# Low passes of a split matrix product moved behind the transposes of the next norm, in a fused two-layer cross-attention and mixture-of-experts kernel

## The chip, the cores and the metric

The kernel runs on one core of a Trainium2 chip. The metric is the device time of one execution in microseconds (us). Each kernel is timed in several runs, and the median counts.

## The reference

The input `x` has 2 x 1024 rows of 256 numbers, the context 2 x 64 rows of 192. Two layers follow one another, each an attention over the context and a feed-forward part, each on a normalised input and with a residual. Cut to what matters here:

```python
x = x + _L0_xattn_ref(_layernorm(x), ctx, ...)   # 16 heads; then relu(out @ W1 + b1) @ W2 + b2
x = x + _L0_ffn_ref(_layernorm(x), ...)          # below
x = x + _L1_xattn_ref(_layernorm(x), ctx, ...)   # one head
x = x + _L1_ffn_ref(_layernorm(x), ...)          # linear

def _L0_ffn_ref(hidden_states, wi, bi, wo, bo, lora_A, lora_B, gate_w, gate_b):
    scores = jax.nn.softmax(hidden_states @ gate_w.T + gate_b)     # 8 experts
    top_v, top_i = jax.lax.top_k(scores, 2)
    val_sum = top_v.sum(axis=-1)
    for e in range(8):
        gate = (top_i == e).sum(axis=-1) * val_sum
        inter = x @ wi.T + bi + (x @ lora_A[e].T) @ lora_B[e].T    # 256 -> 1024
        out = out + gate[..., None] * (relu(inter) @ wo.T + bo)    # 1024 -> 256
    return out
```

All of it is float32.

## The kernel before

The 2048 rows are cut into 8 blocks (`NBLK`) of 256 rows, each of two tiles of 128 rows (`NT` = 2). A block passes through stages that are named by letters: `h` and `a`, the first attention (norm 1, queries, row maxima; then scores, attention, hidden layer and its output), `f`, the expert part (norm 2, gate, hidden layer, output), and `c`, the second layer (norms 3 and 4). One round, `body(a, f, c, h)`, works on four blocks at once: `a` is the round's own block, `f` the block before it, `c` the one before that, and `h` the next one. There are eight rounds, `a` = 0 to 7; round 0 has no `f` and no `c`, round 1 no `c`, and round 7 no `h`. After them come `drain` and `end` for what is left of the last blocks.

Each engine has its own instruction stream, written out by hand in the same round structure; there is no scheduler. The streams meet at semaphores: `pe.wait_ge(S("hidl"), n)` holds back the instruction that follows, and with it all that stands behind it on TensorE. So the order of the lines in `body` of the tensor block is the order on TensorE.

Float32 products are made of three passes over split operands: each operand is stored as a high part of reduced precision (`_h`, type fp32r) and a low part (`_l`, the remainder), and high x high, high x low and low x high are added up in PSUM. The high part is made by ScalarE, the low part by VectorE or GpSimd, as a subtraction.

The names that the change and the steps of the prediction touch:

- `f_out(f, t)` (L474): the second projection of the experts, 1024 -> 256, for tile `t` of block `f`. The activations `HH`, `HL` (`hid_h`, `hid_l` in the profile) are loaded as weights, `wo` streams. `high=True` gives its two passes with `hid_h` (8 matmuls with `wo_h`, 8 with `wo_l`; `NFF` = 8), `low=True` the pass with `hid_l` (8 matmuls). All of it adds up in one PSUM bank, `I_(0)`, half a bank for each tile. The first call waits for `hidh` (ScalarE, L849), the low pass for `hidl` (GpSimd `sum_low`, L1447). The last low pass signals `x2_ps`.
- `second_residual(f)` (VectorE, L1140) waits for `x2_ps` and makes X2; `c_turn(f)` (L490, transposes at L496) waits for X2 and for VectorE's `z`. `f_base(a, 0)` (L450) comes after it. In round 1 (`f == 0`) TensorE also waits for `vv_l` before `c_turn`, a subtraction of VectorE (L1336) that stands between `low(2, a)` and `second_residual(f)` in its queue.
- `a_row_scores(h, t)` (L356): two matmuls of 512 columns for the row maxima of tile `t` of the next block. Those of tile 1 use the same banks as those of tile 0, and so wait for `mx`, VectorE's `row_max(h, 0)` (L1069).
- `a_out(a, half)` (L408): the output of the first layer's hidden part; its end signals `x1_ps`, on which VectorE makes the first residual and the statistics of norm 2 (L1082, L1042 to L1053). GpSimd's `scale(2, a)` then takes the power (L1428) and the product `nmr` (L1432), and ScalarE's `normalise(2, a)` writes `xn`, one tile at a time (L791). `scale(2, a)` stands behind `sum_low(f, 2)` and `sum_low(f, 3)` in GpSimd's queue.
- `transposes(2, a)` (L326): four transposes of `xn`, two for each tile, each pair behind a wait for that tile's `ln2_xh`. ScalarE then makes the high part `xtf_h` (L796), VectorE the low part `xtf_l` (L1057).
- `a_max_transposes(h)` (L365): one transpose of the row maxima; it waits for both row maxima.
- `f_gate(a, h)` (L420, passes at L311 with 136 columns): the gate and the low-rank projections of block `a`, the first user of `xtf_h` and `xtf_l`.
- `experts(a)` on VectorE (L1084 to L1109) ends in `am`, for which `f_lora_transposes` (L434) waits in the next round.

In VectorE's queue the order here is `hidden_sum(f, 3)`, `queries_low(h)`, `row_max(h, 0)`, `first_residual(a)` with the statistics of norm 2, `fourth_residual(c)` (L1183), `row_max(h, 1)`, `low(2, a)`, `second_residual(f)`, statistics of X2, `experts(a)`.

Of the kernel before, what the change touches and what calls it, by code (L numbers as in the profile page):

```python
# [59 lines left out]
def build(nc, io):  # L60
# [157 lines left out]
    with block:  # L218
# [74 lines left out]
        def _(pe):  # L293
# [12 lines left out]
            def passes(parts, chunks, pairs, start, stop):  # L306

                for a, b in pairs:
                    for i, (out, lhs, rhs) in enumerate(parts):
                        for k, c in enumerate(chunks):  # L310
                            last = mm(out, lhs(a, c), rhs(b, c), start=start and (a, b) == pairs[0] and i == 0 and k == 0,  # L311
                                      stop=stop and k == len(chunks) - 1, skip_group_check=True)
                return last

            def w(name, m, n=P):

                return lambda a, c: (WH, WL)[a][name][:, c, m:m + n]

            def x_of(halves, lo=0, n=T):
                return lambda a, c: halves[a][:, c, lo:lo + n]  # L320
# [46 lines left out]
            def a_scores(b, d):  # L367

                if d == 0:
                    if b % BPB == 0:  # L370
                        pe.wait_ge(S(f"ks{b // BPB}"), 16 * 3)
                        pe.wait_ge(S("ks_ind"), b // BPB + 1)
                    for r in range(3):
                        pe.wait_ge(S(f"qstack{r}"), (b + 1) * 16 * GPC)
                    pe.wait_ge(S("mstack"), (b + 1) * NT)
                if d >= 2:
                    pe.wait_ge(S("ex"), b * DPAIRS + d - 1)
                for k in range(2):
                    last = mm(S_(d % 2)[:, k * T:(k + 1) * T], KS[:, b // BPB * PAIRS + 2 * d + k, :],  # L379
                              QS[:, 2 * d + k, :], start=True, stop=True)  # L380
                last.then_inc(S("sc"), 1)

            def a_attend(b, m):

                if m == 0 and b % BPB == 0:
                    pe.wait_ge(S("v0_ready"), b // BPB + 1)
                    pe.wait_ge(S("ld_kept"), 16)
                at = b // BPB * D
                for d in (2 * m, 2 * m + 1):
                    pe.wait_ge(S("ex"), b * DPAIRS + d + 1)  # L390
                    for c in (2 * d, 2 * d + 1):
                        rows = slice(PW * (c % GPC), PW * (c % GPC) + PW)
                        mm(P_(m)[rows, 0:T], v0[:, at + c * PW:at + (c + 1) * PW], EX[:, c, :], start=True, stop=True)  # L393
                        last = mm(P_(m)[rows, T:2 * T], ones_pair, EX[:, c, :], start=True, stop=True)  # L394
                last.then_inc(S("pv"), 1)
# [35 lines left out]
            def f_lora_transposes(b):  # L431
                pe.wait_ge(S("am"), b + 1)
                for k in range(2 * NT):
                    last = nc.tensor.transpose(P_(0)[:, k * P:(k + 1) * P], am[:, k * P:(k + 1) * P], ident)  # L434
                last.then_inc(S("amT"), 1)
# [26 lines left out]
            def f_first(b, u, bank=None):  # L462
                if u == 0:
                    if b == 0:
                        pe.wait_ge(S("lo_w"), 5)
                    pe.wait_ge(S("atl"), b + 1)
                f_lora(b, u, 0, "first_ps", bank)
# [6 lines left out]
            def f_out(b, t, high=True, low=True):  # L474

                if t == 0:
                    if b == 0:
                        pe.wait_ge(S("lo_wp"), 4)
                    pe.wait_ge(S("hidh"), (b + 1) * NDF)
                part = [(I_(0)[:, t * D:(t + 1) * D], x_of((HH, HL), t * P, P), w("wo", 0, D))]  # L480
                if high:
                    passes(part, range(NFF), ((0, 0), (0, 1)), t == 0, False)
                if low:
                    pe.wait_ge(S("hidl"), (b + 1) * NDF)
                    last = passes(part, range(NFF), ((1, 0),), False, True)
                    if t == NT - 1:
                        last.then_inc(S("x2_ps"), 1)
# [15 lines left out]
            def c_scores(b, t):  # L503

                if t == 0:
                    if b == 0:
                        pe.wait_ge(S("gw_l"), 1)
                    split_in(3, b)
                three(T_(t)[:, 0:SY], x_of(XTC, t * P, P), folded_weights(b), range(KC)).then_inc(S("sc1_ps"), 1)
# [108 lines left out]
            def filler(bank, count):  # L618
                for _ in range(count):
                    mm(bank[:, 0:T], zeros[:, 0:P], zeros[:, :], start=True, stop=True)  # L620
# [38 lines left out]
            def body(a, f, c, h):  # L659
                A_, F_, C_, H_ = (v is not None for v in (a, f, c, h))  # L660
                if A_:
                    a_scores(a, 0)
                    a_scores(a, 1)
                if F_:
                    f_lora_transposes(f)
                if C_:
                    c_scores(c, 0)
                    c_scores(c, 1)
                if F_:
                    f_first(f, 0)  # L670
                    f_first(f, 1)
                if A_:
                    a_scores(a, 2)
                if a == 0:
                    filler(I_(0), 2)
                if A_:
                    a_attend(a, 0)
                if F_:
                    f_second(f, 0)
                if f == 0:  # L680
                    fold_means()
                if C_:
                    c_transpose(c)
                if F_:
                    f_second(f, 1)
                if A_:
                    a_scores(a, 3)
                if F_:
                    f_base(f, 2)
                if C_:  # L690
                    c_attend(c)
                if A_:
                    a_attend(a, 1)
                if F_:
                    f_first(f, 2)
                    f_base(f, 3)
                    f_second(f, 2)
                    f_first(f, 3)
                if a == 0:
                    filler(I_(0), 3)  # L700
                    pe.wait_ge(S("v0"), BATCH)
                    transposes(1, h, T_(1))
                    filler(I_(0), 5)
                if A_:
                    a_hidden(a, 0)
                if H_ and a > 0:
                    if f == 0:
                        pe.wait_ge(S("gw"), 1)
                    if C_:
                        pe.wait_ge(S("z"), (c + 1) * NT)  # L710
                    transposes(1, h, T_(1))
                if A_:
                    a_hidden(a, 1)
                if H_:
                    a_queries(h)
                if f == 0:
                    fold_values()
                if F_:
                    f_second(f, 3)
                if A_:  # L720
                    a_out(a, 0)
                if H_:
                    a_row_scores(h, 0)
                if A_:
                    a_out(a, 1)
                if F_:
                    f_out(f, 0)
                if H_:
                    a_row_scores(h, 1)
                if F_:  # L730
                    f_out(f, 1, low=False)
                if a == 0:
                    constant_row()
                    keys1()
                    values1()
                if A_:
                    transposes(2, a, T_(1))
                if a == 0:
                    folded_keys()
                if F_:  # L740
                    f_out(f, 1, high=False)
                if H_:
                    a_max_transposes(h)
                if A_:
                    f_gate(a, h)
                    if a == 0:
                        pe.wait_ge(S("v1"), 1)
                        pe.wait_ge(S("gb"), 1)
                        fold_turn()
                    if F_:  # L750
                        if f == 0:
                            pe.wait_ge(S("vv_l"), 2)
                        c_turn(f)
                    f_base(a, 0)
                    f_base(a, 1)
                elif F_:
                    c_turn(f)
# [860 lines left out]
```

## Time and profile before

| | |
|---|---|
| median of 3 timed runs | 330.58 us |
| lowest and highest | 329.61, 331.83 us |
| time of the profiled execution | 332.24 us |
| its span, first to last instruction | 330.1 us |
| mean granted clock of TensorE | 0.988 |
| busy: TensorE matmuls, weight loads | 314.6 us (95%), 285.6 us (87%) |
| busy: VectorE, ScalarE, GpSimd | 231.2, 173.7, 146.2 us |

The profile is of one execution. PE is TensorE's matmuls, PEld its weight loads, which overlap the matmuls; DVE is VectorE, ACT ScalarE, POOL GpSimd. L311 is line 311 of the kernel; for a helper that many callers share (L302, L311, L458) the tile names tell the stage. A matmul is reported with its whole passage through the array, so matmuls that follow each other overlap in the profile: the distance between the starts of two groups of weight loads tells better than the durations how long a group holds TensorE. The ends of matmuls are modelled.

### The profile page before, as it was taken

The page shows a single profiled execution, that of the slowest core. Times are in us where ns is not written, and L with a number is a line of the kernel's source. Part 1 is how long each engine was busy: PE and PEld are TensorE (multiplying, and loading weights), DVE is VectorE, ACT ScalarE, POOL GpSimd, SP SyncE. Part 2 cuts the span into 40 slices and gives each one's busy share as a digit, 9 for nine tenths or more (in the row PEclk, how much of TensorE's full clock was granted, in tenths as well). Part 3 has the DMA queues.
Part 4 walks back from the last instruction along what each step waited for, and adds up shares of the span by engine and source line. Part 5 has one row for each costly group of instructions (what it writes and reads, how often), then busy time and mean ns, then how long its engine had stood idle before and what let it go on. Part 6 is the DMA issues. An engine that isn't in the chain of part 4 may idle for free.

```text
span 330.1 us, 6479 instructions
## 1 busy us (share of the span) xinstructions
PE 314.6 (95%) x2497; PEld 285.6 (87%) x2497; DVE 231.2 (70%) x644; ACT 173.7 (53%) x355; POOL 146.2 (44%) x150
## 2 busy tenths in 40 slices
PE   7989998999999999999999999999999999999982
PEld 5748897899988999899989997999899988999771
DVE  4746676747878667956886687677786669456766
ACT  3346746572585456564667267635854564534411
POOL 2563681636053723654173607280537234613341
PEclk9989999999999999999999999999999999999997
DMA  8589720003100230013000410032002200000000
GB/s 244 156 247 359 165 82 0 2 9 89 32 3 2 57 92 13 2 26 104 36 0 10 96 57 0 2 85 77 2 0 50 69 13 1 2 0 34 0 34 32
DMA packets 14702, 18.85 MB, mean 57 GB/s; under 512 B 2224, under 2 KB 11312, under 8 KB 14416
## 3 DMA queue, kind: packets, MB, share of 16 engines
q1 hardware_dynamic: 12640, 14.99, 16.9%
q10 hardware_dynamic: 2032, 3.44, 3.0%
q8 instruction: 20, 0.33, 0.4%
q14 instruction: 10, 0.08, 0.1%
HBM read 9.51 MB, written 2.62 MB: 37 GB/s over the span
## 4 chain that ended last, share of the span: by engine, by line
PE 76%; POOL 8%; ACT 5%; DVE 5%; DMA 2%; SPq 2%; issue 1%; DVEq 0%; POOLq 0%; ACTq 0%
PE psI L302 13%; PE psI L458 12%; PE psI L311 9%; PE psP L311 7%; PE psS L311 7%; PE psT L302 4%; POOL hid_l L1447 4%; PE psP L393 3%; POOL hs_l L1441 3%; PE psS L379 2%; PE psT L326 2%; PE psP L394 2%; PE psT L525 2%; ACT qu_h L801 2%; PE psI L620 1%; ACT hs_h L829 1%
## 5 line engine op out<-in xcount | busy, mean ns | idle before, releaser
L1428 POOL TENSOR_TENSOR rs<-ve,mhalf 128x2 f32<-128x2 f32 x30 | 22.3, 745 | 95.3 <-DVE ve L1053 95.3
L1447 POOL TENSOR_TENSOR hid_l<-r,hid_h 128x512 fp32r<-128x512 f32 x32 | 40.8, 1288 | 15.3 <-ACT hid_h L849 15.3
L1132 DVE SCALAR_TENSOR_TENSOR r<-psI,nbi,r 128x256 f32<-128x256 f32 x60 | 25.8, 479 | 25.3 <-PE psI L458 25.2
L458 PE MATMUL psI<-at_h,lb_h 128*128 128x256 f32 x120 | 36.5, 304 | 2.1 <-DVE at_l L1124 1.5
L1441 POOL TENSOR_TENSOR hs_l<-hs,hs_h 128x512 fp32r<-128x512 f32 x16 | 20.8, 1301 | 35.6 <-ACT hs_h L829 35.4
L458 PE MATMUL psI<-at_l,lb_h 128*128 128x256 f32 x120 | 33.9, 282 | 0.0
L458 PE MATMUL psI<-at_h,lb_l 128*128 128x256 f32 x120 | 33.8, 282 | 0.0
L1073 DVE RECIPROCAL rec<-psP 128x256 f32<-128x256 f32 x16 | 28.1, 1753 | 6.5 <-PE psP L394 6.5
L844 ACT ACTIVATE r<-psI,first 128x256 f32<-128x256 f32 x60 | 24.2, 469 | 13.6 <-PE psI L458 13.5
L458 PEld LDWEIGHTS psI<-at_h,lb_h 128*128 128x128 f32 x120 | 22.6, 188 | 8.7 <-issue 5.0
L813 ACT ACTIVATE ex<-psS 128x512 f32<-128x512 f32 x32 | 19.0, 596 | 20.2 <-PE psS L379 20.1
L791 ACT ACTIVATE xn<-xmid,nmr,rs 128x256 f32<-128x256 f32 x16 | 8.8, 598 | 37.1 <-POOL nmr L1432 37.1
L302 PE MATMUL psI<-xtf_h,wi_h 128*128 128x256 f32 x120 | 25.3, 292 | 0.0
L302 PE MATMUL psI<-xtf_h,wi_l 128*128 128x256 f32 x120 | 24.0, 281 | 0.0
L302 PE MATMUL psI<-xtf_l,wi_h 128*128 128x256 f32 x120 | 24.0, 281 | 0.0
L849 ACT ACTIVATE hid_h<-r 128x512 fp32r<-128x512 f32 x32 | 19.5, 628 | 7.7 <-DVE r L1132 7.4
L458 PEld LDWEIGHTS psI<-at_h,lb_l 128*128 128x128 f32 x120 | 22.7, 189 | 0.2
L458 PEld LDWEIGHTS psI<-at_l,lb_h 128*128 128x128 f32 x120 | 22.6, 189 | 0.0
L1069 DVE TENSOR_REDUCE mx<-psS 128x16 f32<-128x1024 f32 x15 | 18.3, 1221 | 5.4 <-PE psS L356 5.4
L1436 POOL TENSOR_TENSOR oa_l<-o,oa_h 128x256 fp32r<-128x256 f32 x16 | 11.8, 737 | 18.7 <-ACT oa_h L818 18.7
L807 ACT ACTIVATE stack<-psP 16x1024 fp32r<-16x1024 f32 x16 | 16.2, 1016 | 7.0 <-PE psP L365 6.8
L302 PEld LDWEIGHTS psI<-xtf_h,wi_h 128*128 128x128 f32 x120 | 18.3, 189 | 0.7
(258 smaller groups left out, 870.6 us busy)
## 6 DMA issues: line engine op xcount, KB each, us to landing
stack<-qu_h SPq DMA_DIRECT2D x60, 64.0 KB, 2.0
xin<-in_x SPq DMA_DIRECT2D x8, 256.0 KB, 2.8
stack<-qu_l SPq DMA_DIRECT2D x30, 64.0 KB, 2.0
out<-x ACTq DMA_DIRECT2D x7, 256.0 KB, 2.0
raw_wi<-in_wi SPq DMA_DIRECT2D x1, 1024.0 KB, 9.1
raw_wo<-in_wo SPq DMA_DIRECT2D x1, 1024.0 KB, 12.4
kv<-in_kv SPq DMA_DIRECT2D x2, 384.0 KB, 8.4
raw_w<-in_w ACTq DMA_DIRECT2D x1, 512.0 KB, 7.5
```

The costliest lines, as they stand in the source:

```text
L302: last = mm(out, lhs(a, c), rhs(b, c), start=start and q == 0 and k == 0, stop=stop and q == 2 and k == n - 1, **kw)
L311: last = mm(out, lhs(a, c), rhs(b, c), start=start and (a, b) == pairs[0] and i == 0 and k == 0, stop=stop and k == len(chunks) - 1, skip_ ...
L458: last = mm(bank[:, k * T:(k + 1) * T], (WH, WL)[x]["lb"][:, 0, f * P:(f + 1) * P], AT[y][:, which, :], start=False, stop=q == 2, skip_gro ...
L813: A(EX[:, 2 * d:2 * d + 2, :], S_(d % 2).rearrange("p (k n) -> p k n", k=2), ACT.Exp, scale=SCALE).then_inc(S("ex"), 1)
L844: last = A(R1[:, f, :], bank[:, k * T:(k + 1) * T], ACT.Relu, bias=cols[:, BI + f:BI + f + 1])
L849: A(HH[:, 2 * u:2 * u + 2, :], R1[:, 2 * u:2 * u + 2, :], ACT.Identity).then_inc(S("hidh"), 1)
L1069: V.reduce_max(MX[:, t, :], ps[:, :].rearrange("p (h k) -> p h k", h=HEADS), AX.X).then_inc(S("mx"), 1)
L1073: V.reciprocal(REC[:, m, :], P_(m)[:, T:2 * T]).then_inc(S("rec"), 1)
L1132: last = V.scalar_tensor_tensor(out=R1[:, f, :], in0=bank[:, k * T:(k + 1) * T], scalar=nbi[:, f:f + 1], in1=R1[:, f, :], op0=MAX, op1=ADD)
L1428: G_.tensor_tensor(rs[:, :], ve[:, :], mhalf[:, :], ALU.pow).then_inc(S(f"ln{j}_rs"), 1)
L1441: G_.tensor_tensor(HS[1][:, two, :], HS32[:, two, :], as32(HS[0][:, two, :]), ALU.subtract).then_inc(S("hsl"), 1)
L1447: G_.tensor_tensor(HL[:, two, :], R1[:, two, :], as32(HH[:, two, :]), ALU.subtract).then_inc(S("hidl"), 1)
```

## The change

In each round that has an `f`, the low pass of tile 0 is taken out of the first call of `f_out` and made in a call of its own behind the transposes of norm 2, directly ahead of the low pass of tile 1. The numbers of matmuls, their operands and their PSUM regions stay the same; each tile's sum keeps the order of its additions. The new call has `t == 0` and so repeats the wait for `hidh` (in round 1 that for `lo_wp` too) in front of the one for `hidl`.

```diff
@@ -724,7 +724,7 @@
                 if A_:
                     a_out(a, 1)
                 if F_:
-                    f_out(f, 0)
+                    f_out(f, 0, low=False)
                 if H_:
                     a_row_scores(h, 1)
                 if F_:
@@ -738,6 +738,7 @@
                 if a == 0:
                     folded_keys()
                 if F_:
+                    f_out(f, 0, high=False)
                     f_out(f, 1, high=False)
                 if H_:
                     a_max_transposes(h)
```

TensorE's queue in a round from 1 to 6, before, from the last matmuls of `a_out` (`w_h`, `hs_l`) to the transposes of X2 (L496). `wo_h,hid_h` and `wo_l,hid_h` are the high passes of one tile, `wo_h,hid_l` is a low pass, L356 the second row scores, L326 the transposes of norm 2:

```order
L311 MATMUL psP<-w_h,hs_l 128x256 x8
L311 MATMUL psI<-wo_h,hid_h 128x256 x8
L311 MATMUL psI<-wo_l,hid_h 128x256 x8
L311 MATMUL psI<-wo_h,hid_l 128x256 x8
L356 MATMUL psS<-kb,qu_h 128x512 x2
L311 MATMUL psI<-wo_h,hid_h 128x256 x8
L311 MATMUL psI<-wo_l,hid_h 128x256 x8
L326 MATMUL psT<-first,xn 128x128 x4
L311 MATMUL psI<-wo_h,hid_l 128x256 x8
L365 MATMUL psP<-first,mx 64x128
L311 MATMUL psP<-ga_h,xtf_h 128x136 x4
```

The same stretch now:

```order
L311 MATMUL psP<-w_h,hs_l 128x256 x8
L311 MATMUL psI<-wo_h,hid_h 128x256 x8
L311 MATMUL psI<-wo_l,hid_h 128x256 x8
L356 MATMUL psS<-kb,qu_h 128x512 x2
L311 MATMUL psI<-wo_h,hid_h 128x256 x8
L311 MATMUL psI<-wo_l,hid_h 128x256 x8
L326 MATMUL psT<-first,xn 128x128 x4
L311 MATMUL psI<-wo_h,hid_l 128x256 x16
L365 MATMUL psP<-first,mx 64x128
L311 MATMUL psP<-ga_h,xtf_h 128x136 x4
```

Eight low matmuls have gone from ahead of L356 to behind L326, and everything between them stands eight matmuls earlier after `a_out`. The next piece is the same place in round 7, which has no row scores and no transpose of maxima, as a difference:

```order
 L311 MATMUL psI<-wo_h,hid_h 128x256 x8
 L311 MATMUL psI<-wo_l,hid_h 128x256 x8
-L311 MATMUL psI<-wo_h,hid_l 128x256 x8
-L311 MATMUL psI<-wo_h,hid_h 128x256 x8
-L311 MATMUL psI<-wo_l,hid_h 128x256 x8
-L326 MATMUL psT<-first,xn 128x128 x4
-L311 MATMUL psI<-wo_h,hid_l 128x256 x8
+L311 MATMUL psI<-wo_h,hid_h 128x256 x8
+L311 MATMUL psI<-wo_l,hid_h 128x256 x8
+L326 MATMUL psT<-first,xn 128x128 x4
+L311 MATMUL psI<-wo_h,hid_l 128x256 x16
```

Between the first high passes and the transposes there are now only the 16 high matmuls of tile 1. The queues of the other engines are the same as before.

## Rows read from the trace of the kernel before

**Rows 1.** Windows of 35 us, core 0: busy (x instructions), TensorE's clock, DMA share, GB/s

```profile
core 0: us, PE busy (x) PEld busy (x) DVE busy (x) ACT busy (x) POOL busy (x), PEclk, DMA share, GB/s
...
136.00:171.00 35.00, 34.94 (x298) 32.70 (x297) 26.19 (x77) 19.95 (x42) 15.82 (x18) 1.00 0.14 39
```

**Rows 2.** Waits of TensorE's weight loads: us in total, times, longest us

```profile
PEld psI L311 <- POOL hid_l L1447: 1.6, 6, 0.3
...
PEld psT L496 <- issue: 0.7, 1, 0.7
```

**Rows 3.** Timeline, round 3: start us, us, engine, line, operation, tiles, count [idle before, releaser]

```profile
146.28 1.22 DVE L1069 TENSOR_REDUCE mx<-psS 128x16 f32<-128x1024 f32 x1
...
146.69 0.70 POOL L1428 TENSOR_TENSOR rs<-ve,mhalf 128x2 f32<-128x2 f32 x1
...
147.36 2.54 POOL L1447 TENSOR_TENSOR hid_l<-r,hid_h 128x512 fp32r<-128x512 f32 x2
...
148.66 1.01 PEld L311 LDWEIGHTS psI<-wo_l,hid_h 128*128 128x128 f32 x8
...
149.94 1.02 PEld L311 LDWEIGHTS psI<-wo_h,hid_l 128*128 128x128 f32 x8 [0.26 <-POOL hid_l L1447]
...
150.14 0.86 POOL L1428 TENSOR_TENSOR rs<-ve,mhalf 128x2 f32<-128x2 f32 x1 [0.25 <-DVE ve L1053]
150.89 0.30 PEld L356 LDWEIGHTS psS<-kb,qu_h 128*128 128x128 f32 x2
...
151.31 1.10 ACT L791 ACTIVATE xn<-xmid,nmr,rs 128x256 f32<-128x256 f32 x2 [4.92 <-POOL nmr L1432]
...
151.66 1.22 DVE L1069 TENSOR_REDUCE mx<-psS 128x16 f32<-128x1024 f32 x1 [0.82 <-PE psS L356]
...
153.26 0.46 PEld L326 LDWEIGHTS psT<-first,xn 128*128 128x128 f32 x4
...
156.16 0.42 PEld L496 LDWEIGHTS psT<-first,x 128*128 128x128 f32 x4
```

**Rows 4.** Timeline, the same place in round 1

```profile
78.23 1.02 PEld L311 LDWEIGHTS psI<-wo_l,hid_h 128*128 128x128 f32 x8
...
79.19 1.01 PEld L311 LDWEIGHTS psI<-wo_h,hid_l 128*128 128x128 f32 x8
...
80.72 1.10 ACT L791 ACTIVATE xn<-xmid,nmr,rs 128x256 f32<-128x256 f32 x2 [4.87 <-POOL nmr L1432]
...
82.50 0.47 PEld L326 LDWEIGHTS psT<-first,xn 128*128 128x128 f32 x4
...
82.96 1.19 PE L311 MATMUL psI<-wo_h,hid_l 128*128 128x256 f32 x8
...
83.88 0.69 DVE L1057 TENSOR_TENSOR xtf_l<-psT,xtf_h 128x512 fp32r<-128x512 f32 x1 [1.74 <-ACT xtf_h L796]
...
84.49 0.68 DVE L1336 TENSOR_TENSOR vv_l<-psT,vv_h 128x512 fp32r<-128x512 f32 x1
...
85.08 0.87 DVE L1140 SCALAR_TENSOR_TENSOR x<-psI,gate,xg 128x256 f32<-128x256 f32 x2
...
86.07 0.42 PEld L496 LDWEIGHTS psT<-first,x 128*128 128x128 f32 x4 [0.66 <-issue]
```

**Rows 5.** Timeline, the same place in round 7, and TensorE's first work after it

```profile
287.85 1.02 PEld L311 LDWEIGHTS psI<-wo_l,hid_h 128*128 128x128 f32 x8
...
289.12 1.02 PEld L311 LDWEIGHTS psI<-wo_h,hid_l 128*128 128x128 f32 x8 [0.25 <-POOL hid_l L1447]
...
290.07 1.03 PEld L311 LDWEIGHTS psI<-wo_h,hid_h 128*128 128x128 f32 x8
...
290.50 1.10 ACT L791 ACTIVATE xn<-xmid,nmr,rs 128x256 f32<-128x256 f32 x2 [4.91 <-POOL nmr L1432]
...
292.00 0.47 PEld L326 LDWEIGHTS psT<-first,xn 128*128 128x128 f32 x4
...
294.91 0.42 PEld L496 LDWEIGHTS psT<-first,x 128*128 128x128 f32 x4
...
298.43 0.42 PEld L434 LDWEIGHTS psP<-first,am 128*128 128x128 f32 x4 [0.23 <-DVE am L1109]
```

## The prediction

> **What bounds the kernel now.** I read the windows view first. In the 35 us of one round in the steady part TensorE is busy for 34.94 us at a granted clock of 1.00, that is the 2.4 GHz of its two levels, and VectorE, ScalarE and GpSimd are at 26.19, 19.95 and 15.82 us [rows 1]. The rounds are one long row of matmuls, so the change can move the end only by the little holes in that row and, at the very end, by the chain behind it. Next I read the list of waits, for TensorE's weight loads (PEld), since a hole shows there first. Two of its rows belong to the stretch that the change touches: six waits for GpSimd's `hid_l`, 1.6 us in all, and one of 0.7 us before the transposes of X2 (L496), put down to "issue" [rows 2]. Then the timeline shows each hole: round 3, which stands for rounds 2 to 6, then round 1, where other VectorE work stands in the way, then round 7, where there is no next tile [rows 3 to 5]. Rounds are counted by `a`, from 0; round 0 has no `f` and is not touched.
>
> **The change, rounds 2 to 6.** Per round 8 matmuls, the low pass of tile 0, leave their place and come back behind the norm's transposes. No instruction goes or comes but one repeated wait on `hidh`, which was met 16 matmuls before; a place with two waits, the transpose of the maxima, costs the row of matmuls nothing before. What moves up by one pass is the second row scores, 16 high matmuls and the four transposes of `xn`.
>
> What goes: the loads of `wo_l` begin at 148.66 and those of the low pass at 149.94, 1.28 us later [rows 3]. In round 1 the same eight take 78.23 to 79.19, 0.96 us, with no wait [rows 4]. So the wait for GpSimd, whose `hid_l` ends at 147.36 + 2.54 = 149.90, costs 0.32 us. In the new place the low pass begins some 2.7 us after 149.90 and can't wait for it.
>
> What comes: from the loads of the second row scores to those of the transposes is 153.26 - 150.89 = 2.37 us [rows 3]. With the low pass gone the row scores begin at 148.66 + 0.96 = 149.62 and the transposes at 151.99. The row scores wait for the first row maximum, which ends at 146.28 + 1.22 = 147.50, so 2.1 us of cover are left. The transposes wait for ScalarE's `xn`, tile by tile: two pieces from 151.31 on, 1.10 us together, so about 0.6 for the first, which ends at 151.91, and 152.41 for the second. After the release of the load at 149.94 by the end at 149.90 I add 0.04 us: 151.95 and 152.45. The first tile comes just in time. The second tile's load was due two loads after 151.99; four loads take 0.46 us, about 0.117 apart, so at 152.22, and it waits 0.23 us. Bounds: 0 if both pieces were ready, which their ends exclude only by tenths, and 0.43 if `xn` comes 0.2 us later than now. I take 0.23, as the durations of all these steps are unchanged in the rows. Net: (0.23 - 0.32) x 5 = -0.45 us.
>
> A rule bears on how to read the first hole. The row of the low pass shows 0.26 us idle, the distance between the loads says 0.32 [rows 3]. The Trainium skill (TensorE: Matmul & The Clock Gate, section LDWEIGHTS (loading the stationary operand)) says that a weight load takes its columns over 1.2 GHz, an estimate of 0.11 us for 128 columns, and the same page says that loads are pulled ahead of running matmuls. By that a wait also lays bare one load, and the distance is the true cost; by the idle column alone the five rounds would give (0.23 - 0.26) x 5 = -0.15 us, and the whole sum 0.3 us less gain.
>
> What follows is covered. ScalarE's high part and VectorE's low part of `xtf` come about 0.8 us earlier, while the loads of the gate matmuls now come after 16 instead of 8 low matmuls. The product of the second projection ends where it did, less the 0.09. GpSimd's and ScalarE's queues keep their order.
>
> **Round 1.** There `hid_l` is in time, and nothing is gained at the first place. The transposes begin at 82.50 - 0.96 = 81.54, the second tile's load is due at 81.77, and `xn` ends at 80.72 + 1.10 = 81.82: with the 0.04 a wait of 0.09 us [rows 4]. But this round has a hole before the transposes of X2: from the loads of the norm's transposes to those of X2 it is 86.07 - 82.50 = 3.57 us, against 156.16 - 153.26 = 2.90 in round 3. It costs 0.67 us. The cause is VectorE's queue: `xtf_l` (from 83.88), then `vv_l` (from 84.49), then the residual X2 (from 85.08, 0.87 us), though the product had ended at 82.96 + 1.19 = 84.15. Now `xtf_l` follows the transposes, 1.38 us behind their first load as before: 81.54 + 0.09 + 1.38 = 83.01. `vv_l` then ends near 84.38, the product at 84.15 + 0.09 = 84.24, so X2 runs from about 84.35 to 85.22. TensorE arrives at 81.54 + 0.09 + 2.90 = 84.53 plus the 0.96 of the returned pass, 85.49. The hole closes with 0.2 us to spare. Net: 0.09 - 0.67 = -0.58 us.
>
> **Round 7.** It has no row scores to put between. The wait for `hid_l` (289.12 - 287.85 - 0.96 = 0.31) goes. The transposes would begin at 287.85 + 0.96 + (292.00 - 290.07) = 290.74, but `xn` ends at 290.50 + 0.60 = 291.10 and 291.60 [rows 5]. The second tile's load, due at 290.97, comes at 291.64: a wait of 0.67, so TensorE is 0.36 us late. Two holes behind it can take that up: 0.1 before X2's transposes (294.91 - 292.00 = 2.91, against 2.90 less one load of about 0.1, since the transpose of the maxima is absent) and 0.23 before those of `am` [rows 5]. The bounds are 0, if VectorE's chain through X2 to `am` stays where it is, and +0.36, if it moves with the product's end as far as TensorE does. I take +0.1, near the lower end, as `xtf_l` stands ahead of that chain and comes earlier than before in round 7 too, by 0.6 us (the second tile's load at 291.64 instead of 292.00 + 0.23).
>
> **Sum.** -0.45 - 0.58 + 0.1 = -0.93 us. The profiled execution has a span of 330.1 and a time of 332.24 us, so it would come to 329.2 and 331.3; it lies 1.7 us above the median of the three timed runs, 330.58. I take the same 0.93 off the median: 329.6 us (329.65).
>
> **Rivals.**
> First, the hole in round 1 stays. X2 needs the product's end, which doesn't move, and 0.2 us is little. For it: VectorE's other work could slip. Against it: the product was over 0.93 us before the residual began. Then only -0.45 + 0.09 + 0.1 = -0.26 is left: 330.3 us.
>
> Second, slower: the wait for `xn` takes the place of the one for `hid_l`, and more. Its place is the second tile's transpose. From 0.32 us on it is dearer than what went, that is if `xn` comes over 0.09 us later than now. For it: GpSimd's power for this norm took 0.86 us beside VectorE's fourth residual and 0.70 us beside a row maximum [rows 3], so that step feels its neighbours, and the change pulls the second row maximum from 151.66 to about 150.85, beside the next product (`nmr`). Against it: the 0.70 us was taken beside just such a row maximum. With `xn` 0.3 us later in rounds 1 to 6: -0.93 + 6 x 0.3 = +0.87, so 331.4 us.
>
> Third, both waits vanish: `xn` and TensorE meet so closely (0.04 and 0.23 us) that a small gain in the norm's chain takes the new wait away. Then -0.32 x 6 - 0.67 = -2.6: 328.0 us. Against it: nothing in that chain, from the first residual to `xn`, is shortened.
>
> Fourth, nothing: the new waits give back exactly what the old ones cost, in round 1 too: 330.6 us. That the change doesn't do what it says I rule out: the order of the instructions shows it.
>
> **How the numbers follow.** Forecast 0.45, first rival 0.17, second 0.13, third 0.08, fourth 0.15, 0.02 for none of them. A difference under 1%, 3.3 us, is about what a measurement of this kernel can't tell from none, and every case lies within it: faster 0.02, same 0.96, slower 0.02. The three timed runs alone span 329.61 to 331.83. The range goes from near the third rival to the second, 328.3 to 331.5, with the scatter of the runs inside it.
>
> **What would show it.** Right: the row of waits "PEld psI L311 <- POOL hid_l" is gone, and one for TensorE's transposes on ScalarE's `xn` (L326 <- L791) has come, some 0.2 us in each of rounds 2 to 6 and 0.6 to 0.7 in round 7. The wait at L496 in round 1 is gone. VectorE's idle time of 0.8 us before the second row maximum shrinks to nearly none. The distance from round to round falls by 0.1 us. Wrong: an `xn` wait over 0.32 us in the middle rounds, an L496 wait that stays, or a distance between rounds that grows, would break the terms in that order; a low pass that still waits for `hid_l` would break the first step.

## The result, and the profile after

The changed kernel took 328.50 us in the median of 6 runs (328.38 to 330.77), beside 330.53 us for the kernel before (6 runs, 329.61 to 331.83). The ratio is 0.9928, with a 95% interval of 0.9900 to 0.9956. So it is faster, by 0.7%, and the medians lie 2.03 us apart, over twice the forecast 0.93. Two later comparisons of the same two kernels gave 0.9966 (0.9943 to 0.9988) and 0.9962 (0.9943 to 0.9981). Over all runs of both on record, without one of the kernel before that took 1053.72 us, the medians are 330.40 us (89 runs) and 328.95 (30), a difference of 1.45 us. That the first comparison shows more than this fits chance, as the repeats below show.

The profiled execution of the changed kernel has a span of 326.2 us, 3.9 less than the profile before. The question is where these 3.9 us lie. The first and the last group of weight loads for the transposes of `am` (L434, one group near the start of each round from round 1 on, the last in `drain`) cut the run into three parts. Of the kernel before, the last one stands in [rows 5] at 298.43; this is the first one, from the timeline:

```profile
52.62 0.46 PEld L434 LDWEIGHTS psP<-first,am 128*128 128x128 f32 x4
```

And the same two of the changed kernel:

```profile
50.19 0.46 PEld L434 LDWEIGHTS psP<-first,am 128*128 128x128 f32 x4
...
294.49 0.42 PEld L434 LDWEIGHTS psP<-first,am 128*128 128x128 f32 x4
```

Between the marks lie 298.43 - 52.62 = 245.81 us before and 294.49 - 50.19 = 244.30 now: 1.51 less. I call this the stretch. Behind it come 31.7 us in both. Ahead of it, in work that the change doesn't touch, the changed kernel's profile is 2.43 us shorter. The run cut into windows shows where most of that comes from. First the kernel before, three windows near the start (busy time by engine, then TensorE's granted clock, DMA share, GB/s):

```profile
16.00:20.00 4.00, 2.79 (x14) 2.21 (x15) 2.82 (x5) 2.03 (x2) 3.92 (x3) 1.00 0.82 202
20.00:24.00 4.00, 3.55 (x26) 1.84 (x24) 1.24 (x6) 1.69 (x3) 1.71 (x3) 0.70 0.89 281
24.00:28.00 4.00, 4.00 (x31) 2.30 (x24) 3.17 (x3) 2.00 (x4) 0.65 (x1) 0.87 0.98 365
```

Then the changed kernel:

```profile
16.00:20.00 4.00, 2.44 (x13) 1.72 (x11) 2.06 (x4) 2.72 (x4) 3.92 (x3) 1.00 0.70 173
20.00:24.00 4.00, 4.00 (x38) 2.40 (x40) 2.80 (x7) 2.18 (x5) 0.92 (x2) 1.00 0.91 299
24.00:28.00 4.00, 4.00 (x24) 3.19 (x21) 2.96 (x5) 1.97 (x5) 1.41 (x2) 1.00 1.00 346
```

In this run of before the clock was at the lower of its two levels, 1.2 GHz, for part of the time from 20 to 28 us, after a window in which TensorE had been busy 2.79 of 4 us; in this run of the changed kernel it stayed at 2.4 GHz, although TensorE had been busy for only 2.44 of the 4 us before. The second profile of the kernel before (`aa_before`, below) kept the 2.4 GHz too, and its first mark stands at 51.02, so the clock is worth about 1.6 of the 2.43 us. The other 0.8 is scatter of the start: the two later profiles of the changed kernel have the full clock there and their first mark at 51.22 and 51.03.

Inside the stretch, the window that answers to [rows 1], and the waits of TensorE's weight loads that answer to [rows 2]:

```profile
136.00:171.00 35.00, 35.00 (x299) 32.73 (x299) 26.34 (x78) 19.96 (x43) 15.86 (x17) 1.00 0.15 39
```

```profile
PEld psT L326 <- ACT xn L792: 2.0, 8, 0.3
```

The waits for `hid_l` and the one at L496 have gone, and this one has come. Seven of its eight are in the changed place, one in each of rounds 2 to 6 and two in round 7; one is from the start of the run, as before. Round 3, which answers to [rows 3]:

```profile
145.43 1.02 PEld L311 LDWEIGHTS psI<-wo_l,hid_h 128*128 128x128 f32 x8
...
146.37 0.31 PEld L356 LDWEIGHTS psS<-kb,qu_h 128*128 128x128 f32 x2
...
148.07 1.09 ACT L792 ACTIVATE xn<-xmid,nmr,rs 128x256 f32<-128x256 f32 x2 [4.92 <-POOL nmr L1433]
...
148.75 0.24 PEld L326 LDWEIGHTS psT<-first,xn 128*128 128x128 f32 x2
...
149.21 0.20 PEld L326 LDWEIGHTS psT<-first,xn 128*128 128x128 f32 x2 [0.23 <-ACT xn L792]
...
149.38 1.96 PEld L311 LDWEIGHTS psI<-wo_h,hid_l 128*128 128x128 f32 x16
...
151.39 0.52 PEld L311 LDWEIGHTS psP<-ga_h,xtf_h 128*128 128x128 f32 x4
...
152.75 0.42 PEld L496 LDWEIGHTS psT<-first,x 128*128 128x128 f32 x4
```

The transposes come in two pairs: the first pair meets its tile just in time, the second waits until `xn` ends at 149.16. Round 1, which answers to [rows 4]:

```profile
79.11 0.52 PEld L326 LDWEIGHTS psT<-first,xn 128*128 128x128 f32 x4
...
80.53 0.69 DVE L1058 TENSOR_TENSOR xtf_l<-psT,xtf_h 128x512 fp32r<-128x512 f32 x1 [1.79 <-ACT xtf_h L797]
...
81.14 0.68 DVE L1337 TENSOR_TENSOR vv_l<-psT,vv_h 128x512 fp32r<-128x512 f32 x1
...
81.81 0.88 DVE L1141 SCALAR_TENSOR_TENSOR x<-psI,gate,xg 128x256 f32<-128x256 f32 x2
...
82.97 0.42 PEld L496 LDWEIGHTS psT<-first,x 128*128 128x128 f32 x4
```

X2 begins 2.70 us behind the first load of the norm's transposes, where it was 2.58 before [rows 4], but with eight more matmuls in between, and L496 has no idle time. Round 7, which answers to [rows 5]:

```profile
283.87 1.03 PEld L311 LDWEIGHTS psI<-wo_l,hid_h 128*128 128x128 f32 x8
...
287.16 0.20 PEld L326 LDWEIGHTS psT<-first,xn 128*128 128x128 f32 x2 [0.34 <-ACT xn L792]
287.65 0.20 PEld L326 LDWEIGHTS psT<-first,xn 128*128 128x128 f32 x2 [0.29 <-ACT xn L792]
...
291.08 0.42 PEld L496 LDWEIGHTS psT<-first,x 128*128 128x128 f32 x4
```

### The profile page after: what moved, and what is told of

Read it like the earlier page. It is cut to its first block, busy times and chain, and to the rows that moved or that the text cites. A ratio compares the mean times of both kernels' runs of the same rounds, so it can differ in the third digit from the quotient of the medians.

```text
span 326.2 us, 6486 instructions
## 1 busy us (share of the span) xinstructions
PE 312.0 (96%) x2497; PEld 284.3 (87%) x2497; DVE 231.3 (71%) x644; ACT 173.2 (53%) x355; POOL 145.4 (45%) x150
## 4 chain that ended last, share of the span: by engine, by line
PE 84%; DVE 5%; ACT 4%; DMA 2%; SPq 2%; POOL 1%; issue 1%; DVEq 0%; POOLq 0%; ACTq 0%
PE psI L302 13%; PE psI L458 13%; PE psP L311 12%; PE psI L311 11%; PE psS L311 7%; PE psT L302 4%; PE psP L393 3%; PE psT L326 3%; PE psS L379 2%; PE psP L394 2%; PE psT L525 2%; PE psS L356 2%; PE psI L620 1%; PE psP L612 1%; DMA xin<-in_x 1%; PE psP L434 1%
```

## The experiments

They are read by the same distances: from the first load of one L434 group to that of the next. The row "round 1" goes from the group in round 1 to the one in round 2, "rounds 2 to 6" is the mean of the next five, "round 7" the last. Every number is worked out from the starts of these groups in the timeline of that kernel.

| kernel | round 1 | rounds 2 to 6 | round 7 | stretch |
|---|---|---|---|---|
| before | 37.16 | 35.06 | 33.34 | 245.81 |
| before, second profile (aa_before) | 37.18 | 35.10 | 33.32 | 245.99 |
| changed | 36.50 | 34.90 | 33.31 | 244.30 |
| changed, second (after_again) | 36.52 | 34.89 | 33.31 | 244.28 |
| changed, third (after_third) | 36.51 | 34.89 | 33.33 | 244.30 |
| low_behind_scores | 37.14 | 34.74 | 33.35 | 244.18 |
| low_ahead_T | 37.14 | 34.74 | 32.99 | 243.81 |
| vv_early | 36.60 | 35.07 | 33.31 | 245.24 |
| resid_later | 36.53 | 34.77 | 33.34 | 243.74 |
| T_earlier | 37.49 | 35.87 | 34.30 | 251.12 |
| ahead_vv | 36.56 | 34.76 | 33.00 | 243.35 |
| only_r1 | 36.50 | 35.05 | 33.29 | 245.06 |
| only_mid | 37.19 | 34.89 | 33.22 | 244.86 |
| only_r7 | 37.17 | 35.10 | 33.40 | 246.06 |

The two profiles of the kernel before agree to 0.04 us in a distance and 0.18 in the stretch; one distance that no edit touched is off by 0.12 (round 7 of `only_mid`). The execution times of one kernel differ by 2 us and more, so the distances decide where a few tenths matter.

**The two kernels against themselves.** `aa_before` is the kernel before, unchanged, `after_again` and `after_third` the changed one.

> The kernel before, unchanged, timed against itself. First theory (holes): the change is worth the 1.5 us that the two profiles show between the first transposes of am (end of round 0) and the last (end of round 7): 245.81 us before, 244.30 after; the other 0.5 to 0.9 us of the timed difference are the start of the run (clock and first instructions), which differs from run to run of one kernel. Then this kernel shows the same spread of starts: some runs near 330.0, some 1.5 to 2.5 us longer with a mean clock of 0.990 or lower, and a ratio within 0.3% of 1; its stretch between the two marks is again 245.8 within 0.1 us. Rival (the change itself speeds the start): all runs of this kernel have the late clock, 0.988, and none of the changed kernel has.

> The changed kernel again. First theory: stretch between the first and the last transposes of am 244.3 us, 1.5 less than before; timed 1.5 to 2.4 us less than before, the part over 1.5 coming with a higher mean clock of its runs. Rival (start): over 2.0 us less in every round, with the first transposes of am 2.4 us earlier than in any run of before.

> The changed kernel a third time, for the size of the timed difference. First theory: stretch 244.3 us, 1.6 less than before, and over all its runs the median is 1.5 to 1.7 us below that of before, both with the same two kinds of starts. Rival (the first measurement's 2.0 to 2.4 us are the true effect, part of it in the start): over 2.0 us less again.

Measured: `aa_before` 330.22 us in the median of 12 runs, ratio 0.9979 (0.9957 to 1.0001); `after_again` 329.26 (12 runs), `after_third` 328.93 (12 runs), both a ratio of 0.997 or 0.996 as given above. The three stretches of the changed kernel lie within 0.02 us of each other. Both kernels have both kinds of starts. Of 83 runs of the kernel before whose clock is known, 16 had a mean granted clock under 0.991, with a median of 331.90 us; of the 30 of the changed kernel 5 had it, with a median of 330.77. (The first profile of the kernel before, with its low clock near 20 us, has a mean of 0.988.) Among the other runs the medians are 330.23 and 328.78 us, again 1.45 apart. So the rival falls: the change doesn't speed the start. With it falls the first comparison's 2.03 us as a size: five of its six runs of the changed kernel happened to lie at 328.38 to 328.58.

**Where the low pass can go.** Two kernels place tile 0's low pass elsewhere. `low_behind_scores`:

```diff
                 if F_:
-                    f_out(f, 0)
+                    f_out(f, 0, low=False)
                 if H_:
                     a_row_scores(h, 1)
                 if F_:
+                    f_out(f, 0, high=False)
                     f_out(f, 1, low=False)
```

> The low pass of tile 0 stands behind the second row scores only, and the transposes of norm 2 keep their place. First theory (the wait for hid_l is what went, 0.34 us a round, and the wait for xn is what came, 0.20): rounds 2 to 6 gain 0.34 each, no wait for xn and none for hid_l; round 1 keeps its hole of 0.67 before the transposes of X2; round 7, which has no row scores, is as before. Sum -1.7 us, stretch between the marks 244.1. Rival (the gain comes from the transposes, which start earlier and feed the gate sooner): nothing is gained, 245.8.

`low_ahead_T` has the added call one line lower, behind `f_out(f, 1, low=False)` and so ahead of the norm's transposes.

> The low pass of tile 0 stands directly ahead of the transposes of norm 2, behind the high passes of both tiles. First theory: rounds 2 to 6 gain 0.34 each, round 1 nothing (its hole of 0.67 stays), round 7 gains 0.31, since the transposes come at 291.7 in the time of before and xn is ready at 291.6. Sum -2.0 us, stretch 243.8: more than the change itself. Rival (earlier transposes are the gain): nothing, 245.8.

Measured: 0.9953 (0.9928 to 0.9978) and 0.9935 (0.9909 to 0.9961), stretches 244.18 and 243.81, against 244.1 and 243.8 expected. Both came to pass round by round: 0.32 to 0.36 us in each of rounds 2 to 6, nothing in round 1, and for `low_ahead_T` 0.33 to 0.35 in round 7. The rival, that the earlier transposes are the gain, falls for these rounds. In `low_ahead_T` the place reads so, in round 3:

```profile
148.94 1.09 ACT L792 ACTIVATE xn<-xmid,nmr,rs 128x256 f32<-128x256 f32 x2 [4.91 <-POOL nmr L1433]
...
149.60 1.02 PEld L311 LDWEIGHTS psI<-wo_h,hid_l 128*128 128x128 f32 x8
150.57 0.46 PEld L326 LDWEIGHTS psT<-first,xn 128*128 128x128 f32 x4
```

None of these loads has idle time. `xn` ends at 150.03, half a microsecond ahead of the transposes.

**The hole in round 1.** `vv_early` is the kernel before, with TensorE's order untouched and one VectorE step moved:

```diff
+                if f == 0:
+                    dve.wait_ge(S("vv_h"), 2)
+                    V.tensor_tensor(VV[1][:, 1:2 * BATCH:2, :], T_(0).rearrange("p (b n) -> p b n", b=BATCH),
+                                    as32(VV[0][:, 1:2 * BATCH:2, :]), SUB).then_inc(S("vv_l"), 1)
                 if A_:
                     low(2, a, XTF, T_(1))
                 if a == 0:
                     low_weights("lb")
-                if f == 0:
-                    dve.wait_ge(S("vv_h"), 2)
-                    V.tensor_tensor(VV[1][:, 1:2 * BATCH:2, :], T_(0).rearrange("p (b n) -> p b n", b=BATCH),
-                                    as32(VV[0][:, 1:2 * BATCH:2, :]), SUB).then_inc(S("vv_l"), 1)
```

> The kernel before, with VectorE's subtraction vv_l of round 1 moved from behind the low part of xtf to ahead of it, where VectorE is idle. First theory: the hole of 0.67 us before the transposes of X2 in round 1 is VectorE's queue (xtf_l, vv_l, X2); with vv_l out of the way X2 starts at the end of the product, 84.2 instead of 85.1 in the time of before, and the hole goes without any change on TensorE: -0.65 us in round 1, nothing elsewhere, stretch between the first and the last transposes of am 245.2. Rival (the hole is the product's end, which the change did not move, or the semaphore of vv_l itself): nothing, 245.8 to 246.0.

Round 1 fell by 0.57 us (37.17 to 36.60), a little less than the expected 0.65, and nothing else moved. In time the kernel can't be told from before (1.000, 0.9977 to 1.0024). The rows of `vv_early`:

```profile
79.99 0.68 DVE L1332 TENSOR_TENSOR vv_l<-psT,vv_h 128x512 fp32r<-128x512 f32 x1
...
80.44 0.47 PEld L326 LDWEIGHTS psT<-first,xn 128*128 128x128 f32 x4
...
81.81 0.69 DVE L1057 TENSOR_TENSOR xtf_l<-psT,xtf_h 128x512 fp32r<-128x512 f32 x1 [1.14 <-ACT xtf_h L796]
...
82.42 0.87 DVE L1140 SCALAR_TENSOR_TENSOR x<-psI,gate,xg 128x256 f32<-128x256 f32 x2
...
83.40 0.42 PEld L496 LDWEIGHTS psT<-first,x 128*128 128x128 f32 x4
```

From the norm's transposes to those of X2 it is now 83.40 - 80.44 = 2.96 us, where it was 3.57, and 2.90 in round 3. VectorE's queue was the cause of the hole. Some 0.06 us of it are left, since X2 follows `xtf_l` and ends only at 83.29.

**What sets `xn`.** `resid_later` is the changed kernel with two steps of VectorE swapped:

```diff
-                if C_:
-                    fourth_residual(c)
                 if H_:
                     row_max(h, 1)
+                if C_:
+                    fourth_residual(c)
```

> The changed kernel, with VectorE's fourth residual moved behind the second row maximum. First theory: GpSimd's power for norm 2 is 0.16 us longer (0.86 against 0.70) because VectorE's fourth residual runs beside it; with a row maximum beside it, it takes 0.70, xn comes 0.16 us earlier, and the wait for xn falls from 0.20 to 0.04 in rounds 2 to 6 and from 0.6 to about 0.45 in round 7: 5 x 0.16 = -0.8 us, up to 0.1 more in round 7, stretch 243.4 to 243.5. Rival (the power's length has nothing to do with its neighbour on VectorE): 0.86 as before, 244.3. Second rival (the later fourth residual delays the low part of xtf and the gate): over 244.3.

Measured: 34.77 us a round instead of 34.90, stretch 243.74, and 0.9947 (0.9929 to 0.9965) against before. In round 3:

```profile
147.58 0.69 POOL L1429 TENSOR_TENSOR rs<-ve,mhalf 128x2 f32<-128x2 f32 x1 [0.25 <-DVE ve L1054]
147.83 1.23 DVE L1070 TENSOR_REDUCE mx<-psS 128x16 f32<-128x1024 f32 x1 [0.33 <-PE psS L356]
148.35 0.20 POOL L1433 TENSOR_TENSOR nmr<-nm,rs 128x2 f32<-128x2 f32 x1
148.58 1.09 ACT L792 ACTIVATE xn<-xmid,nmr,rs 128x256 f32<-128x256 f32 x2 [4.76 <-POOL nmr L1433]
```

The power takes 0.69 us, beside a row maximum, and `xn` begins 1.00 us behind the power's start. In the changed kernel these are 0.86 and 1.16, the power running beside the fourth residual:

```profile
146.73 0.88 DVE L1184 SCALAR_TENSOR_TENSOR x<-y,rs,x 128x256 f32<-128x256 f32 x2
146.91 0.86 POOL L1429 TENSOR_TENSOR rs<-ve,mhalf 128x2 f32<-128x2 f32 x1 [0.26 <-DVE ve L1054]
```

The gain of 0.13 us a round is most of the 0.16 expected; round 7, which has no row maximum to put between, gained nothing. So GpSimd's step does feel its neighbour on VectorE. The swap has a price on the other side. The fourth residual now runs beside GpSimd's `xr`, which also reads two tensors in SBUF:

```profile
148.50 1.29 POOL L1465 TENSOR_TENSOR xr<-xin,kept 128x512 f32<-128x512 f32 x1
...
148.97 1.49 DVE L1184 SCALAR_TENSOR_TENSOR x<-y,rs,x 128x256 f32<-128x256 f32 x2
```

It takes 1.49 us instead of 0.88. The first of its two pieces took 1.10 us (the same or 1.07 in each of rounds 2 to 6), not 0.48, and ended at 150.07, 0.28 us behind `xr`; the second, with `xr` gone, took 0.47. VectorE had slack for it here. The Trainium skill (SBUF — State Buffer, section Who interferes with whom) says that a VectorE instruction with two inputs in SBUF contends with a GpSimd instruction that reads SBUF, and in the summary for kernel authors that the second to issue fully blocks until the first ends. That the two contend, both places agree. Of the blocking, `resid_later` shows as much as this: the piece that started 0.47 us into `xr` didn't end before it, and was held up by 0.62 of the 0.82 us that `xr` still ran. For the power, in the changed kernel, the traces leave it open: it started 0.17 us into the first piece of the residual, which ran 0.31 us more, and became 0.17 us longer, and no trace shows at what moment inside its 0.69 us it reads.

`T_earlier` moves the transposes of the changed kernel up by one more pass, ahead of tile 1's pass of `wo_l` (`which` picks the high passes, `(0, 0)` that of `wo_h` and `(0, 1)` that of `wo_l`):

```diff
-                    f_out(f, 1, low=False)
+                    f_out(f, 1, low=False, which=((0, 0),))
...
                 if A_:
                     transposes(2, a, T_(1))
+                if F_:
+                    f_out(f, 1, low=False, which=((0, 1),))
```

> The changed kernel, with the transposes of norm 2 one more pass up (ahead of tile 1's pass of wo_l). First theory: the norm's chain sets when they can run, so each of the seven rounds loses the pass it moves up, 0.95 us: the wait for xn is 1.15 in rounds 2 to 6 and 1.0 in round 1, sum +6 to +6.6 us, stretch 250.3 to 250.9. Rival (the wait for xn is an artefact of the short gap and is partly made up behind it, since the gate's inputs come earlier): +3 us or less.

Each of the seven rounds became 0.97 to 0.99 us longer, and the stretch 6.8 us, slightly more than expected; its one timed run took 335.72 us. The waits of its weight loads:

```profile
PEld psT L326 <- ACT xn L794: 8.5, 15, 1.3
```

The rival falls: nothing of a wait for `xn` is made up behind it once it is that long.

**The rounds one by one.** Here the change is made in some rounds only, by a condition on `a` at both calls: `a == 1`, `2 <= a <= 6`, `a == 7`.

> The change in round 1 alone. First theory (each round's holes are its own): round 1 takes 36.5 us from the transposes of am to the next instead of 37.2, the others as before (35.06 and 33.3), stretch 245.2 to 245.3. Rival (time won in one round is lost at the next wait): 245.8 or more.

> The change in rounds 2 to 6 alone. First theory: 34.90 us instead of 35.06 in each of the five, 37.2 in round 1 and 33.3 in round 7, stretch 245.0 to 245.1. Rival: 245.8.

> The change in round 7 alone. First theory: the wait for xn of 0.6 us that comes is paid by the wait for hid_l that goes and by the holes behind it, so round 7 takes 33.3 us as before, stretch 245.8 to 246.0. Rival (it costs the 0.3 us by which TensorE is later at the gate): 246.2.

Measured: -0.67 us in round 1, with the others as before; -0.17 to -0.21 in each of rounds 2 to 6; and in round 7 0.06 to 0.08 more. In `only_mid` the untouched round 7 came out 0.10 to 0.12 shorter, so these last hundredths are within what a distance can tell. The parts are each round's own and add up within what the distances can tell. Each of the three was timed once, and the times say nothing by themselves.

**Both steps together.** `ahead_vv` is `low_ahead_T` with the step of `vv_early`.

> The low pass of tile 0 directly ahead of the transposes, and vv_l early: all three holes closed without a new wait. First theory: -2.1 us of the low pass's place and -0.65 of vv_l add up, stretch 243.1 to 243.2, 2.7 us less than before and 1.2 less than the changed kernel; timed 0.8% less than before. Rival (the holes share a cause, so that closing one opens another): 243.8.

The stretch is 243.35 us, 2.5 less than before and 0.95 less than the changed kernel, a little short of the expected 243.1 to 243.2: the 0.06 us before L496 in round 1 are left here as in `vv_early`. The ratio to before is 0.9936 (0.9913 to 0.9959), with a median of 328.52 us in 6 runs. It beats the kernel before beyond doubt; against the changed kernel it is better by its stretch, but the execution times were too few and too scattered to show it.

## Why the prediction was right or wrong

The direction was right, and so was where it would happen. The signs that were named came: the waits for `hid_l` gone, those for `xn` there, L496 in round 1 free, VectorE's second row maximum without its 0.8 us of idle time. The size was too small: -0.93 us, against -1.51 to -1.7 in the stretch, -1.45 in the median of all runs and -2.03 in the first comparison. By the rows of the table the stretch gained 0.59 us more than the sum said: 0.38 of them in rounds 2 to 6, 0.13 in round 7 and 0.08 in round 1. The other half microsecond of the first comparison lies outside the stretch. The steps follow; the first needs these rows of round 3, three of the kernel before and one of the changed kernel:

```profile
153.69 1.02 PEld L311 LDWEIGHTS psI<-wo_h,hid_l 128*128 128x128 f32 x8
...
154.75 0.53 PEld L311 LDWEIGHTS psP<-ga_h,xtf_h 128*128 128x128 f32 x4
...
155.24 0.86 DVE L1140 SCALAR_TENSOR_TENSOR x<-psI,gate,xg 128x256 f32<-128x256 f32 x2
```

```profile
151.59 0.88 DVE L1141 SCALAR_TENSOR_TENSOR x<-psI,gate,xg 128x256 f32<-128x256 f32 x2 [0.58 <-PE psI L311]
```

- **Rounds 2 to 6, -0.45 forecast, -0.8 measured (-0.16 each).** This is the term that failed, and by size alone. It was the difference of two waits of like size, so small slips in both count in full. The wait for `hid_l` cost 0.34 and not 0.32: the eight `wo_l` matmuls take 146.37 - 145.43 = 0.94 us undisturbed, while I had taken 0.96 from round 1. The wait for `xn` cost 0.20 and not 0.23: from the first transpose to the low passes it is 149.38 - 148.75 = 0.63 us, and before, in round 3, 153.69 - 153.26 = 0.43. The rest was a hole of 0.05 us that I had not seen: from the loads of the gate's first pass to L496 it was 156.16 - 154.75 = 1.41 us before and is 152.75 - 151.39 = 1.36 now. Before, X2 ended at 156.10, only 0.06 us ahead of L496, and now at 152.47, 0.28 ahead. The working had taken round 3 as free of holes there. Together 0.34 - 0.20 + 0.05 = 0.19 us a round; from the loads of `wo_l` to L496 it is 7.50 us before and 7.32 now, 0.18 less, and over the whole round 0.16.
- **Round 1, -0.58 forecast, -0.66 measured.** Right. The hole closed and its cause was VectorE's queue, as `vv_early` showed. The same unseen 0.05 was in the 2.90 us against which the hole was measured, and the wait for `xn` cost about 0.05 us, not 0.09 (the loads of the four transposes take 0.52 us instead of 0.47).
- **Round 7, +0.1 forecast, -0.03 and +0.07 measured (whole change and alone).** Right in mechanism: two waits for `xn` of 0.34 and 0.29 us came, 0.63 against 0.67 in the forecast, and the holes behind them, both named, took up what was left. The +0.1 was a choice between bounds, and came out 0.03 to 0.13 too high.
- **The reading of idle time against distance** held. Where the wait for `hid_l` is taken away without a new wait (`low_behind_scores`), a round gains 0.32 to 0.36 us, more than the 0.26 of the idle column. It doesn't hold for every wait: that for `xn` shows 0.23 us idle and cost 0.20.
- **The second rival**, an `xn` that comes later beside the moved row maximum, is out: in the changed kernel the power took 0.86 us and `xn` began 1.16 behind it, where [rows 3] has 0.86 and 1.17. Its argument was half right, though. The step feels its neighbour, but the neighbour that costs is the fourth residual, and it had been there all along.
- **The start of the run** had no term. The sum was set against one profile, whose own time lay 1.7 us above the median; the working noted this and did not ask where it came from. Its stretch of low clock from 20 to 28 us was in the trace. It couldn't have told which share of six runs would have it, but it was a warning that a median over a few runs can move without any cause in the change.

What stays open is why a run has the low clock near 20 us. TensorE's busy time just before doesn't tell the two kinds apart: in the windows from 16 to 20 us it was 2.79 and 2.83 of 4 us in the two profiles whose clock fell (the kernel before and `ahead_vv`), and 2.82 and 2.44 in `aa_before` and the changed kernel, which kept their 2.4 GHz.

## What to carry to other kernels

When a step is moved away from a wait, look at what moves up in its place: here the matmuls that moved up met a second wait over half as long as the first, and with the moved pass one place further up than the change puts it, ahead of the transposes, both were avoided. A forecast that is the difference of two waits needs each of them from the distance between groups in a round that is known to be free of holes. Where execution times scatter by more than the effect, the distance between two marks inside the profile tells changes of 0.1 us apart; measure the unchanged kernel against itself first.

## What the runs showed of the hardware

TensorE's clock near the start isn't the same in every run. In two of the fourteen profiles, of different kernels, it was 0.65 to 0.70 of the full clock from 20 to 24 us and 0.87 to 0.92 from 24 to 28, with a mean of 0.986 and 0.988 over the run; in the other twelve it was 1.00 in both windows, and the mean 0.991 or more. By that mean about one run in five, of either kernel, is of the first kind (21 of 113, under 0.991), and these took 1.7 to 2.0 us longer. That their clock too was low near 20 us is inferred, as these runs have no windows.

GpSimd's power of 128 x 2 numbers takes 0.69 us, but 0.86 while VectorE's fourth residual reads two tensors in SBUF; beside a VectorE maximum over PSUM it keeps its 0.69. The other way round VectorE pays: a piece of that residual took 1.07 to 1.10 us instead of 0.48 when it started half a microsecond into a GpSimd addition of 1.29 us (`resid_later`, five rounds of five).
